# First step's gates placed between the rounds of the matrix exponentials, in two PSUM banks

## The reference

```python
xn = layernorm(x)                                   # norm1
gate, gate_gate = silu(split(xn @ gate_w + gate_b)) # two halves of 256 columns each
u  = (xn * gate) @ state_w + state_b
Bm = gate_gate @ state_w + state_b
delta = softplus(mean(xn @ state_w + state_b))      # one number per token: the step size
y = scan(exp(-delta), delta * Bm * u)               # along the tokens
x = x + y @ out_w + out_b
x = x + mlp(layernorm(x))
...
eo = experts(layernorm(x))                          # top 2 of 8
for i in range(3):
    moe_out = moe_out @ expm(gens[i])               # gens: three 256 x 256 matrices
```

## Time and profile before

| | |
|---|---|
| time, median of 3 runs | 764.22 us |
| profiled execution: time and span | 766.03 us, 764.3 us |
| PE busy | 659.4 us, 86% |
| PE weight loads busy | 489.3 us, 64% |
| DVE busy | 589.9 us, 77% |
| ACT busy | 449.1 us, 59% |
| POOL busy | 243.6 us, 32% |
| mean granted clock of PE | 0.944 of full |

### The profile page before, as it was taken

How to read it: one execution, slowest core, us unless ns; L and a number is a source line. 1 busy time by engine, 2 the same in 40 slices (tenths; PEclk the granted TensorE clock), 3 DMA queues, 4 the chain that set the end, 5 groups by cost and what they waited for, 6 DMA issues and landing times. The chain is left out here.

```text
span 764.3 us, 16165 instructions
## 1 busy us (share of the span) xinstructions
PE 659.4 (86%) x4656; PEld 489.3 (64%) x4682; DVE 589.9 (77%) x1649; ACT 449.1 (59%) x868; POOL 243.6 (32%) x295
## 2 busy tenths in 40 slices
PE   5899999999999989999989986999999999998000
PEld 4667557475564847556464865888888888886000
DVE  5879769897988989898798865667767767765593
ACT  3146482946657284564837343676676676675187
POOL 2003020206336071542606422134334334334042
PEclk9899999999999999999998998899999999999555
DMA  4633242264635336364825643344443444220883
GB/s 139 210 120 55 83 66 57 58 126 169 138 118 111 105 112 139 113 138 147 207 91 168 230 146 94 118 147 139 144 142 105 132 150 145 79 71 17 259 265 138
DMA packets 81777, 99.14 MB, mean 130 GB/s; under 512 B 7728, under 2 KB 71867, under 8 KB 81596
## 3 DMA queue, kind: packets, MB, share of 16 engines
q1 hardware_dynamic: 65308, 68.81, 28.2%
q0 software_dynamic: 16416, 29.67, 16.3%
HBM read 62.42 MB, written 33.68 MB: 126 GB/s over the span
## 5 line engine op out<-in xcount | busy, mean ns | idle before, releaser
L1806 POOL DMA_INDIRECT scratch_ys<-ye,place x78 | 82.6, 1059 | 161.9 <-ACT ye L1852 150.0
L58 PE MATMUL bank<-words 128*128 128x512 bf16 (+1 forms) x567 | 107.6, 343 | 5.0 <-DVE logits L1021 2.1
L58 PE MATMUL up<-xe_s,words 128*128 128x256 bf16 x936 | 111.0, 276 | 0.9 <-DVE xe_s L1943 0.9
L58 PE MATMUL down<-words,h_s_e 128*128 x936 | 110.2, 274 | 0.8 <-DVE yb L1927 0.8
L58 PEld LDWEIGHTS up<-xe_s,words 128*128 x936 | 92.5, 99 | 12.7 <-issue 1.3
L58 PEld LDWEIGHTS down<-words,h_s_e 128*128 128x128 bf16 x936 | 91.3, 98 | 13.5 <-issue 1.1
L58 PE MATMUL bank<-xn_s,mlp_w 128*128 128x512 bf16 x368 | 86.5, 387 | 3.7 <-DVE xn_s L746 2.9
L58 PEld LDWEIGHTS bank<-words 128*128 128x128 bf16 x576 | 55.0, 98 | 51.7 <-issue 5.6
L475 POOL DMA_INDIRECT scratch_zs<-rows,pos x64 | 72.6, 1135 | 44.7 <-DVE pos L1071 25.9
L58 PE MATMUL bank<-mlp_w,shared 128*128 128x256 bf16 x768 | 86.5, 273 | 0.0
L58 PEld LDWEIGHTS bank<-mlp_w,shared 128*128 128x128 bf16 x768 | 74.9, 98 | 10.7 <-issue 0.4
(11 more groups left out here) (244 smaller groups left out, 1203.3 us busy)
## 6 DMA issues: line engine op xcount, KB each, us to landing
xr<-scratch_zs SPq DMA_DIRECT2D x39, 264.0 KB, 2.8
words<-scratch_ys SPq DMA_DIRECT2D x16, 514.0 KB, 8.8
scratch_abel<-staged SPq DMA_DIRECT2D x8, 514.0 KB, 4.6
abel_all<-scratch_abel SPq DMA_DIRECT2D x8, 514.0 KB, 5.5
x_in<-in_x SPq DMA_DIRECT2D x8, 512.0 KB, 4.6
words<-in_out_b_row SPq DMA_DIRECT2D x8, 512.0 KB, 3.3
x_res<-in_mlp_b_row SPq DMA_DIRECT2D x8, 512.0 KB, 3.5
words<-in_x POOLq DMA_DIRECT2D x8, 512.0 KB, 7.6
```

Source lines behind the costliest of these rows:

```text
L58: last = nc.tensor.matmul(dst, lhs(a, k), rhs(b, k), start=start and n == 0, stop=stop and n == total - 1)
L1806: nc.gpsimd.indirect_dma_start(out=ys_dram[:, :], out_offset=bass.IndirectOffsetOnAxis(ap=place[:, k, s:s + 1], axis=0), in_=ye[:, k % 2, ...
```

## The change

Four things are moved, on PE, ACT and DVE, and the first step gets banks of its own for it:

- PE: `exponential_round` is cut into `round_turns` and `round_products`. `turn1(0)` goes between round 1's turns and its products, `first_gates(0)` (12 matmuls, c = 0 and 1) between rounds 1 and 2, `gates(0, ...)` (12 matmuls, c = 2 and 3) between round 2 and the loop, and `step_size(0)` (6 matmuls) behind the loop, ahead of the wait for the loop's last update.
- Banks: step 0's gates use banks 6 and 7 in turn (`gate_bank`), its step size bank 7 (`size_bank`). So PE waits for the silu of c = 0 ahead of c = 2, of c = 1 ahead of c = 3, and for all four ahead of the step size; late product 1, which uses bank 7, waits for the magnitudes.
- ACT: `norm1(0)` goes ahead of the copies of round 2's turned matrices, the four silus and `gate_heads(0)` ahead of the loop.
- DVE: `norm1_split(0)` goes ahead of the combinations that follow round 1, `gate_product(0)` and `gate_split(0)` to where it was. `gate_tails(0)` stays behind the loop.

```diff
+        def gate_bank(i, c):
+            return bank[6 + c % 2 if i == 0 else c]
+        def size_bank(i):
+            return bank[7 if i == 0 else 4]
...
             weight_heads((0, 1))
-            for r in (1, 2):
-                for s in range(GENS):
-                    turned_copy(r * GENS + s, s)
-            weight_heads((2,))
+            for s in range(GENS):
+                turned_copy(GENS + s, s)
             act.wait_ge(vec_in, 16 * len(vectors))
             norm1(0)
+            for s in range(GENS):
+                turned_copy(2 * GENS + s, s)
+            weight_heads((2,))
+            silus(0, range(0, 2 * KC))
+            gate_heads(0)
             act.wait_ge(sq_r, 6)
...
             weight_tails((0,))
+            norm1_split(0)
             for s in range(GENS):
                 dve.wait_ge(prod_done, GENS + s + 1)
...
                 stt(X[:, s], mat(3 + s), scaled[:, 4:5], X[:, s]).then_inc(mat_r, 1)
-            norm1_split(0)
+            gate_product(0)
+            gate_split(0)
             dve.wait_ge(vec_in, 16 * len(vectors))
...
                     if c >= KC:
                         wait(pe, x1_r, 2 * (i - 1) + c - KC + 1)
+                        if i == 0:
+                            pe.wait_ge(g_r, c - KC + 1)
...
+                if i == 0:
+                    pe.wait_ge(g_r, 2 * KC)
+                split_product(nc, size_bank(i)[:, :], lambda s, k: mean_w[:, s, k], lambda s, k: xn_s[:, s, k], KC)\
                     .then_inc(zz_done, 1)
...
-            exponential_round(0, A, A)
-            exponential_round(GENS, A2, U, True)
-            exponential_round(2 * GENS, L, U, True)
+            round_turns(0, A)
+            round_products(0, A)
+            round_turns(GENS, A2)
             turn1(0)
+            round_products(GENS, U, True)
+            pe.wait_ge(w_tail, 1)
+            first_gates(0)
+            round_turns(2 * GENS, L)
+            round_products(2 * GENS, U, True)
+            gates(0, range(KC, 2 * KC))
             pe.wait_ge(sq_r, 6)
             squarings = pe.value_load(sq_i[0:1, 0:1], min_val=SQ_MIN, max_val=SQ_MAX)
             with pe.Fori(SQ_MIN - 1, squarings) as k:
-                exponential_round(k * GENS + (3 * GENS - LATE), X, X)
+                round_turns(k * GENS + (3 * GENS - LATE), X)
+                round_products(k * GENS + (3 * GENS - LATE), X)
+            pe.wait_ge(mean_done, 6)
+            step_size(0)
             pe.wait_ge(mat_r, squarings * GENS + (3 * GENS - LATE))
```

More of the change, by code:

```diff
@@ L529, in late_copies, with silus, gate_heads @@
                     nc.scalar.activation(aT[:, n % GENS], mat(5), ACT.Copy).then_inc(late_copied, 1)
+            def silus(i, cs):
+                for c in cs:
+                    act.wait_ge(gate_done, 4 * i + c + 1)
+                    wait(act, g_tail if c < KC else gg_tail, i)
+                    dst = g if c < KC else gg
+                    nc.scalar.activation(dst[:, c % KC], gate_bank(i, c)[:, :], ACT.Silu,
+                                         bias=gate_b[:, c:c + 1]).then_inc(g_r, 1)
+            def gate_heads(i):
+                act.wait_ge(g_r, 4 * i + 4)
+                wait(act, b_done, 2 * i)
+                nc.scalar.activation(gg_s[:, 0], gg[:, :, :], ACT.Copy).then_inc(gg_head, 1)
             for s in range(GENS):
@@ L550, in token_weights @@
                         .then_inc(tok_head, 1)
[L552 to L563, removed]
             def norm2(j):
@@ L575, in magnitudes @@
                 wait(act, delta_r, i)
-                nc.scalar.activation(az[:, :], bank[4][:, :], ACT.Abs, bias=mean_b[:, :]).then_inc(az_r, 1)
-                nc.scalar.activation(rz[:, :], bank[4][:, :], ACT.Relu, bias=mean_b[:, :]).then_inc(rz_r, 1)
+                nc.scalar.activation(az[:, :], size_bank(i)[:, :], ACT.Abs, bias=mean_b[:, :]).then_inc(az_r, 1)
+                nc.scalar.activation(rz[:, :], size_bank(i)[:, :], ACT.Relu, bias=mean_b[:, :]).then_inc(rz_r, 1)
             def w1_heads(es):
@@ L638, in _ @@
             for i in range(BATCHES):
-                silus(i, range(0, KC))
                 if i > 0:
+                    silus(i, range(0, KC))
                     norm2(i - 1)
-                silus(i, range(KC, 2 * KC))
-                gate_heads(i)
+                    silus(i, range(KC, 2 * KC))
+                    gate_heads(i)
                 if i == 0:
@@ L767, in norm1_split, with gate_product, gate_split, gate_tails @@
                 split(xn_s, xn[:, :, :], xn_head, xn_tail, i)
+            def gate_product(i):
+                dve.wait_ge(g_r, 4 * i + 2)
+                nc.vector.tensor_tensor(g[:, :, :], g[:, :, :], xn[:, :, :], ALU.mult).then_inc(xg_r, 1)
+            def gate_split(i):
+                dve.wait_ge(xg_r, i + 1)
+                wait(dve, u_done, 2 * i)
+                split(g_s, g[:, :, :], g_head, g_tail, i)
+            def gate_tails(i):
+                dve.wait_ge(gg_head, i + 1)
+                nc.vector.tensor_tensor(gg_s[:, 1], gg[:, :, :], gg_s[:, 0], ALU.subtract).then_inc(gg_tail, 1)
             def square_copy(s):
@@ L932, in norm2_split @@
                 split(xn2_s, xn2[:, :, :], xn2_head, xn2_tail, j)
[L934 to L945, removed]
             def deltas(i):
@@ L1132, in _ @@
                 j = i - LAG
-                gate_product(i)
+                if i > 0:
+                    gate_product(i)
                 if j >= 0:
@@ L1137, in _ @@
                     norm2_split(i - 1)
-                gate_split(i)
+                if i > 0:
+                    gate_split(i)
                 gate_tails(i)
@@ L1300, in first_gates @@
                 for c in range(KC):
-                    part_product(nc, bank[c][:, :], weight(c), rows_of_step, KC, ((0, 0), (1, 0)), True, False)
+                    part_product(nc, gate_bank(i, c)[:, :], weight(c), rows_of_step, KC, ((0, 0), (1, 0)), True, False)
                 pe.wait_ge(xn_tail, i + 1)
                 for c in range(KC):
-                    part_product(nc, bank[c][:, :], weight(c), rows_of_step, KC, ((0, 1),), False, True)\
+                    part_product(nc, gate_bank(i, c)[:, :], weight(c), rows_of_step, KC, ((0, 1),), False, True)\
                         .then_inc(gate_done, 1)
@@ L1311, in gates @@
                         wait(pe, x1_r, 2 * (i - 1) + c - KC + 1)
-                    split_product(nc, bank[c][:, :], lambda s, k: gate_w[:, s, k, c * P:(c + 1) * P],
+                        if i == 0:
+                            pe.wait_ge(g_r, c - KC + 1)
+                    split_product(nc, gate_bank(i, c)[:, :], lambda s, k: gate_w[:, s, k, c * P:(c + 1) * P],
                                   lambda s, k: xn_s[:, s, k], KC).then_inc(gate_done, 1)
@@ L1322, in step_size @@
                     pe.wait_ge(eb_r, 1)
-                split_product(nc, bank[4][:, :], lambda s, k: mean_w[:, s, k], lambda s, k: xn_s[:, s, k], KC)\
+                if i == 0:
+                    pe.wait_ge(g_r, 2 * KC)
+                split_product(nc, size_bank(i)[:, :], lambda s, k: mean_w[:, s, k], lambda s, k: xn_s[:, s, k], KC)\
                     .then_inc(zz_done, 1)
@@ L1520, in product, with round_turns @@
                 last.then_inc(done, 1)
-            def exponential_round(n, lhs, rhs, paired=False):
+            def round_turns(n, lhs):
                 for s in range(GENS):
@@ L1528, in exponential_round, with round_products @@
                     turn_mat(lhs[:, s], s, turned)
+            def round_products(n, rhs, paired=False):
                 for s in range(GENS):
@@ L1542, in late_product @@
                 pe.wait_ge(late_copied, n + 1)
+                if n == 1:
+                    pe.wait_ge(az_r, 1)
+                    pe.wait_ge(rz_r, 1)
                 wait(pe, late_r, n - 1)
@@ L1580, in _ @@
                 j = i - LAG
-                if i == 0:
-                    pe.wait_ge(w_tail, 1)
-                first_gates(i)
                 if i > 0:
+                    first_gates(i)
                     turn2(i - 1)
[L1586 to L1589, removed]
+                    gates(i, range(KC, 2 * KC))
+                    step_size(i)
                 if i == 1:
```

## The result

The changed kernel takes 757.97 us, the median of 6 runs (757.29 to 760.3), the kernel before 764.05 (6 runs, 762.52 to 765.09). The ratio is 0.9927, with a 95% interval of 0.9914 to 0.9940: 6.1 us faster, where 4.7 were forecast. The profiled executions differ by 5.7 us in time (766.03 and 760.3) and by 5.8 in span. The busy times are nearly the same as before: the same work with less waiting.

A forecast was written before the change was run, and what follows sets the result against it. Behind 130 us PE bounds the kernel, so its idling in the start was to be cut: −5.0 us, +0.3 for handshakes, sum −4.7, from the median 764.22 to 759.5; own range 758.0 to 760.9, wider 757.3 to 762.5.

The forecast's parts named there:

- First turns at no cost, only together with the gates: PE's 4.91 us hole ahead of round 1's products: eight turns cost nothing there and take 1.04 us off the path.
- Split of xn ahead of DVE's combinations costs 0.1 at most: DVE after round 1: first combination 0.5 us late, idle 0.46 us takes all but 0.1 of it.
- Round 3 at full clock, new wait 0.9: PE, round 3: products take 5.18 us instead of 6.76, after 0.9 us of waiting for ACT's first copy.
- Rival A: Half clock stays on round 3's products, behind the new wait; price 1.6 us, time 761.1; chance 0.15.
- the 43.5 that would have spoken against the forecast: Sign on PE: the forecast is wrong if round 3's products start after 43.5 us.
- Step size as cover for DVE's last update, 1.0: PE behind the loop: six matmuls, 1.25 us, cover DVE's last update, which cost 1.01 us before.
- Sum on PE 5.0, on ACT 5.4: Late turns begin 5.0 us earlier on PE; magnitudes begin 5.4 us earlier on ACT.
- The lesser of the two holds from the projection on: From the projection on, the smaller lead, PE's 5.0 us rather than ACT's 5.4, is what stays.
- Handshakes 0.3: Loop entry, a register load, now amid work on ACT and PE: costs 0.3 us, bounds 0 and 0.7.
- Rival B: Kernel before, round 3: runs without the half clock at 39.7 have 1.0 us less to gain; 760.5 us; chance 0.17.
- What follows stays: After 54 us all three engines do the same in the same order, so the 5.0 us stays.

The follow-up runs named there:

- the late head: Changed kernel with ACT's head of gg behind the loop's copies instead of ahead of them; 758.71 us, ratio 0.9927 to the kernel before.
- the clock kept in both starts: Hole ahead of round 1's products filled with unused matmuls: eight in the changed kernel, 757.04 us; ten in the kernel before, 761.59 us.
- the last gates back: Changed kernel with gates c = 2 and 3, their silus and the head of gg back behind the loop; 759.45 us, ratio 0.9934.
- once the clock is held: Twelve unused matmuls behind norm2's last turn, in both kernels: kernel before 762.48 us, ratio 0.9954; changed kernel 758.49 us, ratio 0.9913.

## Why the prediction was right

- *First turns at no cost, only together with the gates:* right (2.44 us of waiting when alone).
- *Split of xn ahead of DVE's combinations costs 0.1 at most:* right; the split ends 4.1 us after round 1's products start (4.3 by the forecast), and DVE still has 0.38 of the 0.46 us of waiting behind it. That so much is left is partly luck: the product that ends the wait comes 0.22 later too, as round 1's products ran 0.22 us longer in this execution.
- *Round 3 at full clock, new wait 0.9:* 5.45 us for the products, a wait of 1.04; the cause is shown by the late head, which takes 0.72 of it away. Rival A didn't come: the clock stayed at 1.00 behind the wait. The products start at 43.47, only just below the 43.5 that would have spoken against the forecast, since this profile is 0.75 us late by then.
- *Step size as cover for DVE's last update, 1.0:* 0.96.
- *Sum on PE 5.0, on ACT 5.4:* 4.98 and 5.31.
- *"The lesser of the two holds from the projection on":* wrong. It was the greater, 5.30. The projection waits for y, which hangs on the magnitudes by ACT and DVE; PE had 0.36 us of idling there and now has none. A lead of 0.3 fitted into that.
- *Handshakes 0.3:* there were none. The loop's entry cost nothing on ACT or PE; the copy at 42.84 follows the head at once, so the 0.6 us that the prediction names for a register load isn't seen here either.
- *Rival B* (before loses less in executions without the half clock at 39.7): the gain with the clock kept in both starts is 4.20, against 5.1 from one profile to the other, so about 0.9 of the gain is that clock; the distance from round 3's turns to the late turns gives 1.16; 1.0 was forecast. The sum counted 0.26 us of it as a wait: the turns ahead of round 3's products take 2.07 us before and 1.81 in the profile with the last gates back, both with a wait for X, since the clock falls within them at 39.7 and not behind them. In all three profiles of the kernel before whose hole isn't filled the half clock is there, so it belongs to the gain of most executions; for those at 0.954 that is open.
- *"What follows stays":* the mis-sized term. In order it was right, the stretch up to the last batches is the same to 0.1 us once the clock is held. But the half clock in PE's late waits fell otherwise: 317.76 before, 316.77 and 315.01 after, against 315.4 with it held. That is 1.0 to 2.8 us that the forecast had at zero, and 0.3 to 1.5 more from there to the end (356.75 before, 356.49 and 355.22 after). I had read this stretch only for its busy share and not for its clock, though 0.98 over 570 us is 23 us at half clock.
- *Range and luck:* 757.97 lies 1.5 us below the forecast of 759.5 and just outside the forecast's own range (758.0 to 760.9); it lies in the wider one (757.3 to 762.5), whose low end was reckoned from no new wait, no handshakes and 1 us of scatter. There were indeed no handshakes, which is 0.3, but the new wait came, so the time isn't there for the reasons given: the other 1 us lies behind the start, where no term foresaw it. That it stayed within the range is luck to this extent.

So of the 6.1 us about 5.1 arise at the start, some 4 of order and 0.9 to 1.2 of clock at round 3. The remaining 1.0 lies behind it; the profiles show the clock in the late waits as what varies there, and that it makes up just this 1.0 in the medians is argued, not measured, since the interval of the ratio alone allows 4.6 to 6.6 us in all. Why the shift makes the half clock rarer there in most executions, and not merely different, wasn't settled: it may hold for this offset alone, and the executions that weren't profiled show only their mean clock.

## What to carry to other kernels

Independent products belong where the engine waits for somebody else's result, and one sees their worth by counting the waits that they replace, not their own length: twelve matmuls of 2.6 us were worth 0.8 in the distances. When order moves by a few us, look at every later wait behind which the clock falls, and compare kernels with those waits filled before giving a remainder to the change.

## What was not expected of the hardware

The same kernel falls into groups of time by its mean granted clock: in one series 766.2 to 767.2 us at 0.943 and 760.9 at 0.954 for the kernel before, nothing else changed. The same wait of 1.57 us ahead of round 3's turns had the half clock behind it in three profiles and not in a fourth, in which the hole at 16 us was filled. And work without use can be worth its place: twelve matmuls in a wait of 2.9 us made the kernel before 2.7 us faster (ratio 0.9954, 0.9939 to 0.9969), ten in the hole at 16 us made it 3.3 faster (761.59 against 764.91, ratio 0.9963, 0.9944 to 0.9982). For the changed kernel no such gain is clear of the scatter.
